# Reading two stacks of LoRA matrices one adapter per transfer, in a two-layer kernel on one core

## The reference, cut to what matters

```python
def _L0_ffn_ref(x, gate, kernel, bias, lora_A, lora_B, lora_A_shared, lora_B_shared):
    base_out = jnp.matmul(x, kernel) + bias
    x_flat = x.reshape(b, -1, x.shape[-1])                 # 8 groups of 256 rows
    A_eff = jnp.einsum('bn,nri->bri', gate, lora_A)        # lora_A: 16 x 32 x 1024
    B_eff = jnp.einsum('bn,nor->bor', gate, lora_B)        # lora_B: 16 x 1024 x 32
    Ax = jnp.einsum('bri,bti->btr', A_eff, x_flat)
    delta_flat = jnp.einsum('bor,btr->bto', B_eff, Ax)
    Ax_s = jnp.einsum('ri,bti->btr', lora_A_shared, x_flat)
    delta_flat = delta_flat + jnp.einsum('or,btr->bto', lora_B_shared, Ax_s)
    return base_out + delta_flat.reshape(base_out.shape)
x = x + _L0_ffn_ref(_L0_cond_ref(x, ...), ...)
x = x + _L1_ffn_ref(_L1_cond_ref(x, ...), ...)
```

## Time and profile before

| | us |
|---|---|
| median of 3 runs | 794.06 |
| the profiled execution, whole | 797.76 |
| its span, first to last instruction | 796.0 |
| PE busy | 778.0 (98%) |
| PE weight loads busy | 659.6 (83%) |
| DVE busy | 523.1 (66%) |
| ACT busy | 215.6 (27%) |
| GpSimd busy | 81.7 (10%) |
| DMA, mean rate over the span | 165 GB/s |

### The profile page before, as it was taken

One profiled execution on the slowest core, in us unless ns is written; L12 is line 12 of the kernel. 1 busy time (PEld: TensorE's weight loads), 2 busy tenths in 40 slices (PEclk: granted clock), 3 DMA queues, 4 the chain that ended last, 5 costly groups with the idle time before them and its releaser, 6 DMA issues.

```text
span 796.0 us, 10457 instructions
## 1 busy us (share of the span) xinstructions
PE 778.0 (98%) x3933; PEld 659.6 (83%) x3933; DVE 523.1 (66%) x620; ACT 215.6 (27%) x254; POOL 81.7 (10%) x53
## 2 busy tenths in 40 slices
PE   7979999999999999989999999999999999999998
PEld 6867888888888899968888888888888888888886
DVE  4876646255353479987777759877765896555552
ACT  5541101001000032243333337333333731111110
POOL 2430351422313000000000000000000000000000
PEclk9999999999999999999999999999999999999999
DMA  8939665545475899244455134288862764444441
GB/s 228 312 142 269 151 158 130 132 113 145 116 169 123 181 277 235 80 133 132 133 147 157 40 130 135 79 230 236 238 245 81 253 223 159 166 174 161 158 174 64
DMA packets 90604, 131.47 MB, mean 165 GB/s; under 512 B 11048, under 2 KB 70296, under 8 KB 87624
## 3 DMA queue, kind: packets, MB, share of 16 engines
q1 hardware_dynamic: 87664, 130.72, 56.1%
q10 hardware_dynamic: 2792, 0.11, 0.2%
q0 software_dynamic: 112, 0.17, 0.1%
HBM read 79.24 MB, written 51.72 MB: 165 GB/s over the span
## 4 chain that ended last, share of the span: by engine, by line
PE 84%; DVE 7%; DMA 6%; SPq 2%; ACT 1%; issue 1%; DVEq 0%
PE ps L1823 37%; PE ps L1564 27%; PE ps L1883 19%; DMA raw<-in_L_ffn_kernel 3%; DVE cr L1268 2%; DVE cf L1274 1%; DVE cf L1260 1%; DMA a_scratch<-w_a_f 1%; DVE wk_lo L1055 1%; DVE c_st L1274 1%; DMA lora_b_scratch<-lb_c_lo 1%; DMA lb<-lora_bs_scratch 1%; DVE w_a_f L1218 1%; ACT wk_hi L803 1%; SPq L528 0%
## 5 line engine op out<-in xcount | busy, mean ns | idle before, releaser
L1823 PE MATMUL ps<-cr,w_s_hi 128*128 128x512 f32 x512 | 159.0, 392 | 2.5 <-ACT s L909 2.5
L1823 PE MATMUL ps<-cr,w_a_hi 128*128 128x512 f32 x384 | 118.4, 389 | 0.0
L1823 PEld LDWEIGHTS ps<-cr,w_s_hi 128*128 128x128 f32 x512 | 96.5, 189 | 23.5 <-issue 3.3
L1823 PE MATMUL ps<-cr,w_s_lo 128*128 128x512 f32 x256 | 100.3, 392 | 0.0
L1823 PEld LDWEIGHTS ps<-cr,w_a_hi 128*128 128x128 f32 x384 | 71.9, 188 | 15.1 <-issue 0.2
L1137 DVE TENSOR_TENSOR x_t<-ps,x_t 128x1024 f32<-128x1024 f32 x16 | 19.5, 1223 | 96.7 <-PE ps L1564 96.7
L1564 PE MATMUL ps<-wk_hi,y_hi 128*128 128x512 f32 x256 | 80.5, 395 | 0.7 <-DVE wk_lo L1055 0.5
L1564 PE MATMUL ps<-wk_lo,y_hi 128*128 128x512 f32 x256 | 79.0, 390 | 0.0
L1564 PE MATMUL ps<-wk_hi,y_lo 128*128 128x512 f32 x256 | 78.9, 389 | 0.0
L737 POOL TENSOR_TENSOR x_t<-x_in,f_bias 128x1024 f32<-128x1024 f32 x16 | 62.0, 3879 | 152.0 <-DMA x_scratch<-x_t 152.0
L1823 PE MATMUL ps<-cr,w_a_lo 128*128 128x512 f32 x192 | 74.7, 389 | 0.0
(11 more groups left out here) (173 smaller groups left out, 1251.8 us busy)
## 6 DMA issues: line engine op xcount, KB each, us to landing
x_scratch<-x_t SPq DMA_DIRECT2D x128, 64.5 KB, 2.2
x<-x_scratch SPq DMA_DIRECT2D x32, 258.0 KB, 6.9
x_in<-in_x SPq DMA_DIRECT2D x16, 512.0 KB, 6.7
r_scratch<-r_t SPq DMA_DIRECT2D x16, 512.0 KB, 3.3
h_scratch<-s SPq DMA_DIRECT2D x32, 256.0 KB, 2.3
h_f<-h_scratch SPq DMA_DIRECT2D x8, 1024.0 KB, 5.9
res<-r_scratch SPq DMA_DIRECT2D x16, 512.0 KB, 5.0
raw<-in_L_ffn_w SPq DMA_DIRECT2D x56, 128.0 KB, 4.4
```

The lines of the kernel that those rows point to most:

```text
L1823: last = pe.matmul(o, l, r, start=first and q == 0 and n == 0, stop=q == 3 and n == 2, skip_group_check=True)
```

## The change

A and B are each read as 16 transfers of 128 KB, one adapter each, in place of 4 transfers of 512 KB each: 32 transfers for 8. One transfer reads one contiguous stretch of HBM and writes 16 partitions, where before it took 4 KB pieces from 8 adapters and wrote all 128. In A a partition gets two rows of 4 KB (rows r and r + 16), in B one piece of 8 KB. Partition p now holds row p % 16 of adapter p // 16, and `sel` and `m_x` follow that order; their sizes and the count of instructions on PE, DVE, ACT and GpSimd stay. All 16 transfers of A are issued ahead of `load_x(0)`, where half of A used to come behind `load_x(1)`. PE's `la_part` waits for the whole of A at its first call. B stays in its place behind `load_wk(4)`.

```diff
-        sel = at("sel", [NLORA, NH, NX, 8], 173.25)
+        sel = at("sel", [NLORA, NH, 8, NX], 173.25)
-        la_in = [sem(f"la_in{c}") for c in range(2 * NH)]
+        la_in = sem("la_in")
-            la_v = lora_a.rearrange("(h n) (k r) i -> k h r n i", h=NH, r=NX)
-
-            def load_la(k, h):
-                sp.dma_start(la_raw[:, NH * k + h, :], la_v[k, h]).then_inc(la_in[NH * k + h], 16)
-
-            lb_v = lora_b.rearrange("(h n) (x z o) r -> h z x n (o r)", h=NH, x=NX, z=2)
-
-            def load_lora_b(h):
-                for z in range(2):
-                    q = slice(z * NX // 2, (z + 1) * NX // 2)
-                    sp.dma_start(lb_raw[:, h, q].rearrange("p q m -> p (q m)"), lb_v[h, z]).then_inc(lb_in, 16)
-
-            load_la(0, 0)
-            load_la(0, 1)
+            def load_lora_a(n):
+
+                h, p0 = n // 8, n % 8 * NX
+                sp.dma_start(la_raw[p0:p0 + NX, :, :].rearrange("p (k h) i -> p h k i", h=NH)[:, h],
+                             lora_a[n].rearrange("(k r) i -> r k i", r=NX)).then_inc(la_in, 16)
+
+            def load_lora_b(n):
+
+                h, p0 = n // 8, n % 8 * NX
+                sp.dma_start(lb_raw[p0:p0 + NX, h, :, :].rearrange("p q m -> p (q m)"),
+                             lora_b[n].rearrange("(x o) r -> x (o r)", x=NX)).then_inc(lb_in, 16)
+
+            for n in range(NLORA):
+                load_lora_a(n)
             load_x(0, 0)
             load_wk(0)
             load_x(1, 1)
-            load_la(1, 0)
-            load_la(1, 1)
...
-            load_lora_b(0)
-            load_lora_b(1)
+            for n in range(NLORA):
+                load_lora_b(n)
...
-            link(dve.reduce_max(m_x[:, :], ident[:, :].rearrange("p (x n) -> p x n", x=NX), AX.X))
-            dve.tensor_copy(sel[:, :, :, :], ident[0:NLORA, 0:NLORA].rearrange("g (h n) -> g h n", h=NH).unsqueeze(2)
-                            .to_broadcast([NLORA, NH, NX, 8])).then_inc(sel_made, 1)
+            link(dve.reduce_max(m_x[:, :], ident[:, :].rearrange("p (n x) -> p x n", x=NX), AX.X))
+            dve.tensor_copy(sel[:, :, :, :], ident[0:NLORA, 0:NLORA].rearrange("g (h n) -> g h n", h=NH).unsqueeze(3)
+                            .to_broadcast([NLORA, NH, 8, NX])).then_inc(sel_made, 1)
...
                 pe.wait_ge(gate_made, 1)
-                for h in range(NH):
-                    pe.wait_ge(la_in[NH * k + h], 16)
+                pe.wait_ge(la_in, 16 * NLORA)
...
-            pe.wait_ge(lb_in, 16 * 2 * NH)
+            pe.wait_ge(lb_in, 16 * NLORA)
```

More of the change, by code:

```diff
@@ L1603, in _ @@
                 last = mm(bank(1)[:, h * NG:(h + 1) * NG],
-                          sel[:, h].rearrange("g x n -> g (x n)"), gate_t[:, :], True, True)
+                          sel[:, h].rearrange("g n x -> g (n x)"), gate_t[:, :], True, True)
             last.then_inc(gate_mm, 1)
```

## The result

The changed kernel takes **803.59 us** (median of 4 runs, 801.68 to 805.29) where the kernel before took 794.14 on the same chip (4 runs, 793.2 to 794.59): a ratio of 1.0111, 95% interval 1.008 to 1.0141. The difference is 9.5 us. The forecast was 801.4, with 793.8 to 807.3 as its range and 0.77 on slower.

What follows compares the result with a forecast made beforehand. PE's row-tile products from 71.04 us bound the end, the start reaching them through A_eff, GpSimd's run and `z_taken`. 7.9 + 1.7 - 2.3 = +7.3 us on 794.06 gives 801.4 us, range 793.8 to 807.3.

Steps and rivals of the forecast that it cites:

- rate of A; rate of B: DMA into 16 partitions: 135 GB/s, so 15.5 us each for A and for B; bounds 107 to 165.
- PE's first A product later by: PE, ready at 14.33 us, stands until all of A is in at 22.3: +7.9 us.
- half clock behind it: After PE's wait for A its granted clock drops to 0.50, slowing the 16 small products: +1.7 us.
- given back by GpSimd's L731: DVE's two `y_rest` of tile 0 no longer meet GpSimd's L731, over by then: -2.3 us.
- B, by kernel block 5: Block 5, behind B, is split by 52.0, before GpSimd's run ends at 54.7: B's slowness hidden by 2.7 us.
- upper bound of 165: DMA of A at 165 GB/s takes 12.7 us: +5.1, about +4.5 us after the clock and DVE terms.
- The quarter: Added to the 107 GB/s because consecutive transfers go to different partitions and overlap somewhat, and are half as long.
- SP's bound of 205 GB/s: SP's issue of 16 A transfers, 0.60 us plus 0.04 each, takes 10.2 us; the bound if data were faster.
- Rival 1: Source, not narrowness, slowed A and B; contiguous reads run at SP's issue rate: 793.9 to 796.7 us; chance 0.25.
- Rival 2: DVE's `wk_lo_part(5)` gets in ahead of GpSimd's L737; PE's 5.07 wait and slow clock go: 787.3 us; chance 0.05.
- Rival 3: Worse than the bound: the rate's halving is no floor, or PE loses its clock twice: from 808 us; chance 0.07.

Runs made afterwards that it cites:

- the draw told above: First profile of the kernel before, nothing changed: its first product of `lb` and `z` came 4.0 us later than in the second; spans 796.0 against 793.4.
- the filler: Changed kernel plus 40 small matmuls, results unused, on PE directly before its first wait for A: 808.71 us, ratio 1.0159.

## Why the prediction was right, and where its steps were not

Slower was right, and so was the mechanism in the main: transfers to 16 neighbouring partitions move at some 0.6 of the rate before, PE stands for A, and the start carries over to the end. The forecast of +7.3 us fell short of +9.5. Step by step, with the second profiles of both kernels (spans 802.7 and 793.4, 9.3 apart), because the first one of before held the draw told above:

| step | forecast | measured: first pair of profiles; second pair |
|---|---|---|
| rate of A; rate of B (range over both) | 135; 135 GB/s | 149 to 165; 131 to 148 |
| PE's first A product later by | 7.9 us | 6.35; 5.0 |
| half clock behind it | +1.7 | +2.1; +1.6 |
| given back by GpSimd's L731 | -2.3 | 0; 0 |
| B, by kernel block 5 | 0 | second pair +1.4 |
| second clock drop, and 0.52 more of a wait for `lb` | 0 | second pair +1.1 |

The second pair's values add up: 5.0 + 1.6 + 1.4 + 1.1 = 9.1 us at the first product of `lb` and `z` (76.14 against 67.05), and 9.3 at the end.

**The rate.** A's lay above the value taken (149 and 163 to 165 in the two traces of the change, 169 to 171 with the filler), B's on both sides of it (131 to 148). The forecast's upper bound of 165 was worked out from no row. The quarter that the prediction added for an overlap of transfers to different partitions is not borne out: with neighbours in the queue 64 partitions apart the rates stayed at 147 and 143. The reason that the prediction gave, that the rate falls with the number of partitions written, is wrong: spread over every eighth partition, 16 of them run at 207 with time to spare. SP's bound of 205 GB/s was also mis-sized: a narrow transfer takes SP 0.46 us with its gap, not 0.64.

**What was given back.** This is the first step that failed. It moved DVE with PE and left L731 where it was. But ACT makes `wk_hi` of block 0 behind its `y_bias` copy, and that copy waits for PE's `yb_r` product behind the A products. ACT at 25.32, GpSimd at 27.75 and DVE at 28.22 all moved by 8.5 us together, and `y_lo` still took 3.60. The rows of before that would have told it are these, ACT's and GpSimd's; the prediction went by DVE's alone.

```profile
16.85 0.38 ACT L830 ACTIVATE y_bias<-ps 128x256 f32<-128x256 f32 x1 [1.75 <-PE ps L1564]
...
19.28 2.89 POOL L731 TENSOR_TENSOR wk_lo<-raw,wk_hi 128x1024 fp32r<-128x1024 f32 x1 [13.40 <-ACT wk_hi L803]
```

**B's cover.** This is the second. The prediction gave B 2.7 us of cover, because `wk_lo_part(5)` seemed to hang on the end of GpSimd's run. One profile of a race was taken for a rule. By that rule block 5 was still covered in the changed kernel: ACT had split it at 53.90 and GpSimd's run ended at 57.46. But DVE ran from 53.94 to 56.21, in the midst of that run, and PE waited for it. There is a cover, of another kind: `z_taken` hangs on GpSimd's second L737 as long as `wk_lo_part(5)` ends early enough. In the second pair GpSimd's L737 moved by 6.6 us (38.17 to 44.81) and the end of `wk_lo_part(5)` by 10.5 (43.94 to 54.45), so block 5 came 3.9 us late against it; `z_taken` moved by 8.0 (48.58 to 56.59), so 2.5 of the 3.9 were covered and 1.4 cost time.

**Errors that offset each other.** PE's delay for A was put 1.5 to 2.9 us too large, because A came faster than 135 GB/s. Against it stand the 2.3 us that weren't given back and the 1.4 and 1.1 us behind B that the sum lacks. The 1.1 is what is left of a half clock that cost 1.6 us from the last B product on: PE's wait for `x_in`, 1.09 us before, took up most of it, and the wait for `lb` added 0.52. That the total missed by only 2.2 us is partly luck.

**The rivals.** Rival 1 fell: reading contiguously did not free the narrow transfers. Its reason has some truth in the other direction, for the kernel before: its 16 x 8 shape holds A at 240 where a plain one has 415, but that gain is worth nothing (ratio 0.9997), since PE reaches A's products at 13.9 to 14.6 us either way, without a wait. The Trainium skill's rule on large power-of-two pitches ("DMA: Bandwidth & Descriptors", "Latency and other measured facts") is not seen here at 64 KB, which ran at 414, and no run has its 512 KiB. The prediction quoted that rule's 207 GB/s as a loss; the Trainium skill calls 214 the full rate of those copies, so its loss at 512 KiB is small. Rival 2 was in the main already the state of the kernel before in its second profile (a wait of 1.72 us, no clock drop), and the 1.72 hang on GpSimd, so there was little to win. Rival 3's second clock drop did come, 3.4 us long behind the wait for `z_taken`, and costs under 1.1 us.

**What the change costs, by its parts.** Many transfers cost 2 to 3 us (797.3 with 1 KB pieces to all partitions, 797.98 spread); for the spread ones SP's issue is the bound, for the others it is not the whole reason; that each of them goes to 16 neighbouring partitions costs the other 6 to 8 (9.5 less those). That both kernels with 128 KB transfers also wait for A (2.71 and 3.25 us) and then run at a lower granted clock is in their 2 to 3 (the first A products take 3.75 and 3.23 us, and 2.05 to 2.50 in the two profiles of before).

## What to carry to other kernels

Where a load is cut by objects that fill a few neighbouring partitions each, either fetch several objects in one transfer over all partitions, or lay each one over the partitions in steps; then count SP's time per issue. Before a slack is booked, follow every engine of the pair back to what starts it: an engine that seems free may be moved by the same wait. And a stall that comes from two engines meeting by chance wants a second profile before a cover is built on it, and in it the durations of the short instructions behind the stalled one too.

## What the runs showed of the hardware that was not expected

- At 16 partitions per transfer the choice of partitions alone changes the rate: 131 to 171 GB/s for neighbours, 207 (share 0.67) to 217 (share 0.99) for every eighth.
- SP's issue of a 128 KB transfer depends on its target: 0.423 us to 16 neighbouring partitions, 0.592 to 16 spread ones, and 0.04 between two in both cases.
- A 128-partition load whose source is 16 times 8 pieces of 4 KB ran at 236 to 263 GB/s, plain ones (128 rows at one pitch) at 403 to 415, and at 414 with steps of 64 KB in the source.
- DVE's low part of kernel block 5 took 2.27 to 6.40 us from run to run: 2.27 where it began after GpSimd's second L735 had ended, 4.43 where it began in the first L737, 6.40 where it began in the second and the short gathers behind it went ahead too. A cast of z that takes 0.28 to 0.35 us otherwise took 2.84 to 2.86 us in seven profiles and ended 0.14 to 0.16 us after the GpSimd instruction that was running.
